# Setup folded into the first units, half groups shifted by one unit, and one PSUM ring of four, in a four-layer graph network on one core

## The reference, cut to what matters

```
x = _layernorm(x + L0(x, adj, W, a_src, a_dst))           # attention, 4 heads: softmax(mask(leaky_relu(si + sj))) @ (xW), elu
x = _layernorm(x + L1(x, adj, weight, w_ih, w_hh, b...))  # 3 rounds: m = h @ weight[i]; aggr = A^T m; h = gru_cell(aggr, h)
x = _layernorm(x + L2(x, adj, weight, bias))              # for r in 1..4: (adj == r) @ x @ weight[r], summed, + bias
x = _layernorm(x + L3(x, adj, W, a))                      # attention, 1 head, elu
```

## Time and profile before

| what | value |
|---|---|
| median of 3 runs | 2815.49 us (2813.47 to 2816.87) |
| the profiled execution, its own time | 2813.75 us |
| its span in the trace | 2811.9 us |
| TensorE: busy, share, matmuls | 2686.6 us, 96%, 15577 |
| VectorE / ScalarE / GpSimd busy | 76% / 59% / 45% |
| mean granted TensorE clock | 0.975 |

### The profile page before, as it was taken

The page is one execution under the profiler, slowest core; times in us unless marked ns, Lnnn a source line. Parts: engine busy times, 40 slices in busy tenths (PEclk is TensorE's granted clock), DMA queues, the critical chain, the costliest instruction groups (busy, mean ns, idle before and its releaser), DMA issues.

```text
span 2811.9 us, 48614 instructions
## 1 busy us (share of the span) xinstructions
PE 2686.6 (96%) x15577; PEld 2315.8 (82%) x15577; DVE 2126.9 (76%) x5138; ACT 1663.4 (59%) x4164; POOL 1257.9 (45%) x1351
## 2 busy tenths in 40 slices
PE   3799999999999999999999999999999999999984
PEld 2678888888888888888888888888888888888873
DVE  6466787777788777878778777877777788777754
ACT  0455666666566666666566666656666666666542
POOL 0134544454445445444544544444444444444442
PEclk8699999999999999999999999999999999999995
DMA  7000000000000000000000000000000000000000
GB/s 202 19 20 18 18 24 22 27 24 26 22 21 24 22 28 24 26 22 18 27 22 27 24 26 18 22 24 26 27 24 24 20 22 22 28 28 18 13 10 16
DMA packets 97276, 75.29 MB, mean 27 GB/s; under 512 B 6624, under 2 KB 92768, under 8 KB 96992
## 3 DMA queue, kind: packets, MB, share of 16 engines
q1 hardware_dynamic: 77296, 54.28, 6.7%
q10 hardware_dynamic: 19696, 17.44, 1.9%
...
## 4 chain that ended last, share of the span: by engine, by line
PE 75%; DVE 11%; issue 4%; ACT 2%; POOL 2%; POOLq 0%; DVEq 0%; ACTq 0%
PE psum L757 45%; PE psum L618 9%; PE psum L674 5%; PE psum L654 3%; PE psum L792 3%; PE psum L745 3%; PE psum L744 2%; PE psum L663 2%; PE psum L633 2%; DVE ht_h L1085 2%; DVE y_t L1031 2%; DVE stats L1008 2%; DVE y_t L1132 1%; ACT x L932 1%; DVE moments L1012 1%
## 5 line engine op out<-in xcount | busy, mean ns | idle before, releaser
L1166 POOL TENSOR_SCALAR rstd<-moments 128x2 f32<-128x2 f32 x256 | 78.8, 308 | 999.5 <-DVE moments L1012 999.1
L757 PE MATMUL psum<-ht_h,whh_h 128*128 128x512 f32 x1152 | 481.3, 418 | 0.0
L757 PE MATMUL psum<-ag_h,wc_h 128*128 128x512 f32 x1152 | 478.2, 415 | 0.0
L757 PE MATMUL psum<-ht_h,whh_l 128*128 128x512 f32 x1152 | 456.0, 396 | 0.0
L757 PE MATMUL psum<-ag_l,wc_h 128*128 128x512 f32 x1152 | 455.6, 395 | 0.0
L757 PE MATMUL psum<-ht_l,whh_h 128*128 128x512 f32 x1152 | 455.5, 395 | 0.0
L757 PE MATMUL psum<-ag_h,wc_l 128*128 128x512 f32 x1152 | 454.1, 394 | 0.0
L1221 POOL TENSOR_TENSOR ht<-ht,g_n 128x512 f32<-128x512 f32 x192 | 265.2, 1381 | 151.2 <-ACT g_n L920 148.7
L757 PEld LDWEIGHTS psum<-ht_h,whh_l 128*128 128x128 f32 x1152 | 216.6, 188 | 52.8
L757 PEld LDWEIGHTS psum<-ag_h,wc_l 128*128 128x128 f32 x1152 | 216.3, 188 | 53.0
L757 PEld LDWEIGHTS psum<-ht_l,whh_h 128*128 128x128 f32 x1152 | 217.7, 189 | 38.6
...
## 6 DMA issues: line engine op xcount, KB each, us to landing
adj_i<-in_adj_dram SPq DMA_DIRECT2D x128, 128.0 KB, 2.1
...
```

The source lines that it names most:

```text
L757: last = mm(dst, s, m, start=(first and k == 0), stop=(last_part and k == len(flat) - 1))
```

## The change

- **Setup.** The separate block is gone. Its loads, transposes, products and splits are steps (`prep_*`, `load_*`, `scan`, `flag`, `learn`) of the same list as everything else. They use banks 4 to 7 before the GRU does (ring `prep`). The products are cut into pieces of one bank. `adj` is scanned in 32 pieces instead of 8, with a ring of 3 buffers; 7 of the pieces stand ahead of the first GRU step, 25 behind it. The flag is worked out and read just ahead of the first `rel_rest`.
- **Halves.** Half k holds units 2k-1 and 2k instead of 2k and 2k+1. There are 33 halves; the first and the last hold one unit (two graphs), and all their GRU steps work on 256 columns instead of 512.
- **Orders.** `HALF` is a new order of the same steps, and `FIRST` and `LAST` list the steps of the two ends by hand.
- **PSUM.** `light` and `misc` become one ring `light` of four banks, taken in the order of the list.

```diff
-SLOTS = {"light": 2, "misc": 2, "adj": 2, "x": 2, "xt": 1, "wh": 2,
+SLOTS = {"light": 4, "adj": 2, "x": 2, "xt": 1, "wh": 2,
-         "adjg": 1, "nodes": 1, "agg": 1, "adjf": 1, ... "x1": 3}
+         "adjg": 1, "nodes": 1, "agg": 1, "prep": 4, "scan": 3, "adjf": 1, ... "x1": 3}
-    "gru_load": ("adjg",), "gru_nodes0": ("nodes",), "gru_turn0": ("misc",),
-    "gru_agg": ("misc",), "gru_turn": ("misc",), "gru_fin": ("misc", "yf"),
+    "gru_load": ("adjg",), "gru_nodes0": ("nodes",), "gru_turn0": ("light",),
+    "gru_agg": ("light",), "gru_turn": ("light",), "gru_fin": ("light", "yf"),
+    "prep_hh": ("prep",), "prep_ih": ("prep",), "prep_wl": ("prep",), "prep_w3": ("prep",), "prep_mul": ("prep",),
+    "scan": ("scan",), "flag": ("light",),
...
+FIRST = """
+prep_first()  load_first()  pre_load(0)  load_ih()  att_xt(pre,0)  pre_load(1)  att_wh(pre,0,0)  att_wh(pre,0,1)
...
+gru_agg(0,0,0)
+gru_agg(0,0,1)  att_wh(pre,2,0)  att_wh(pre,2,1)  att_scores(pre,2,0)
...
+LAST = """
...
+gru_in(-1,2,1)  rel_y1(-2)  gru_new(-1,2,1)  rel_rest(-2)  att_prob(post,-3)  att_store(post,-4)  gru_fin(-1,0)  rel_norm(-2)
...
-    return [(name,) + kind + (2 * k + a[1],) + a[2:]]
+    u = 2 * k - 1 + a[1]
+    return [(name,) + kind + (u,) + a[2:]] if 0 <= u < 2 * halves - 2 else []
...
-    HALVES = B // 4
+    HALVES, UNITS = B // 4 + 1, B // 2
...
-        LIGHT, MISC = psum[:, 0:2, :], psum[:, 2:4, :]
+        LIGHT, PREP = psum[:, 0:4, :], psum[:, 4:8, :]
...
+        def units(k):
+            return [u for u in (2 * k - 1, 2 * k) if 0 <= u < UNITS]
...
+            def prep_mul(l, j):
+                i = take(pe, "prep", "prep_mul", l, j)
+                prepped(pe, "prep_wl", l)
+                prepped(pe, "prep_ih", j)
+                for n, c in enumerate((j,) if j < C else range(C)):
+                    cols = slice(0, 2 * D) if j < C else slice(2 * D, G3)
+                    dst = PREP[:, i, :] if j < C else PREP[:, i, n * D:(n + 1) * D]
+                    for e in range(C):
+                        last = mm(dst, wlT[:, l, e, c * P:(c + 1) * P], ihT[:, e, cols], start=(e == 0), stop=(e == C - 1))
+                last.then_inc(s_prep_ps, 1)
...
             def gru_hn(k, l, c):
 
                 if l == 0:
-                    pe.wait_ge(s_ht0_l, 2 * k + 2)
+                    if k == 0:
+                        pe.wait_ge(s_prep_lo, len(PIECES))
+                    pe.wait_ge(s_ht0_l, 2 * k + 2)
...
-                accumulate(HN_PS, gate_terms(rows_of(2, c), whh_h, whh_l, ht_h[k % 2], ht_l[k % 2]), True, True).then_inc(s_ph, 1)
+                accumulate(HN_PS[:, nodes_of(k)], gate_terms(rows_of(2, c), whh_h, whh_l, ht_h[k % 2], ht_l[k % 2], nodes_of(k)), True, True).then_inc(s_ph, 1)
```

More of the change, by code:

```diff
@@ L73 @@
 HALF = """
[L74 to L77 removed]
+rel_h1(-2,0)
+gru_z(-1,1,1)
+gru_in(-1,1,1)  rel_split(-2,1)  rel_adjt(-2,1)  rel_y1(-2,0)  rel_rest(-2,0)
+gru_agg(0,0,0)
+gru_agg(0,0,1)  att_scores(pre,1,0,0)  att_scores(pre,1,0,1)  att_store(post,-3,0)
+gru_hn(0,0,0)  rel_norm(-2,0)  gru_new(-1,1,0)  rel_mask(-2,1)
@@ new lines @@
+gru_agg(0,1,0)
+gru_agg(0,1,1)
+gru_hn(0,1,0)  scan(14)  scan(15)
+gru_rzh(0,1,0)  att_norm(pre,2)
+gru_r(0,1,0)
+gru_z(0,1,0)  scan(16)  scan(17)  gru_nodes0(1)  gru_turn0(1,0)
+gru_in(0,1,0)  gru_turn0(1,1)
+gru_hn(0,1,1)  att_scores(pre,3,0)
+gru_rzh(0,1,1)  gru_n(0,1,0)  gru_new(0,1,0)
+gru_r(0,1,1)
+gru_z(0,1,1)  att_scores(pre,3,1)
+gru_in(0,1,1)
+gru_agg(1,0,0)
+gru_agg(1,0,1)
+gru_hn(1,0,0)  scan(18)  scan(19)  scan(20)  gru_n(0,1,1)  gru_new(0,1,1)  gru_split(0,1)  att_prob(pre,3)
+gru_rzh(1,0,0)  pre_load(4)
@@ new lines @@
+gru_in(1,1,0)
+gru_hn(1,1,1)
+gru_rzh(1,1,1)  gru_nodes0(2)  gru_turn0(2,0)  scan(30)  gru_turn0(2,1)  gru_n(1,1,0)
+gru_r(1,1,1)  att_scores(pre,5,0)  scan(31)
+gru_z(1,1,1)
+gru_in(1,1,1)
+gru_agg(2,0,0)
+gru_agg(2,0,1)  att_scores(pre,5,1)  rel_split(0)  rel_adjt(0)
+"""
+LAST = """
+rel_mask(-4)  gru_new(-2,1,0)
+gru_hn(-1,0,0)
+gru_rzh(-1,0,0)
+gru_r(-1,0,0)  gru_n(-2,1,1)  gru_new(-2,1,1)
+gru_z(-1,0,0)
+gru_in(-1,0,0)
+gru_hn(-1,0,1)
+gru_rzh(-1,0,1)  rel_norm(-5)  att_xt(post,-5)  gru_split(-2,1)  rel_h1(-4)
@@ L132, in placed, with from_end @@
     k = t + a[0]
-    if not 0 <= k < halves:
-        return []
     if name.startswith("gru"):
-        return [(name, k) + a[1:]]
-    return [(name,) + kind + (2 * k + a[1],) + a[2:]]
+        gone = name in ("gru_turn", "gru_fin", "gru_norm") and (k, a[-1]) in ((0, 0), (halves - 1, 1))
+        return [] if gone or not 0 <= k < halves else [(name, k) + a[1:]]
+    u = 2 * k - 1 + a[1]
+    return [(name,) + kind + (u,) + a[2:]] if 0 <= u < 2 * halves - 2 else []
 def program_order(halves):
-    return [s for t in range(-2, halves + 3) for step in half_steps(HALF) for s in placed(step, t, halves)]
+    def from_end(step):
+        name, a = step[0], step[1:]
+        at = 1 if name.startswith("att") else 0
+        return (name,) + a[:at] + (a[at] + (halves if name.startswith("gru") else 2 * halves - 2),) + a[at + 1:]
+    first, last = steps_of(FIRST), [from_end(s) for s in steps_of(LAST)]
+    apart = set(first) | set(last)
+    middle = [s for t in range(-2, halves + 3) for step in steps_of(HALF) for s in placed(step, t, halves)]
+    scans = [("scan", i) for i in range(SCANS) if ("scan", i) not in apart]
+    out = []
+    for s in middle:
+        if s == ("rel_rest", 0) and ("flag",) not in apart:
+            out += [("flag",), ("learn",)]
+        if s not in apart:
+            out.append(s)
+            if s[0] in ("gru_hn", "gru_rzh", "gru_r", "gru_z") and scans:
+                out.append(scans.pop(0))
+    assert not scans
+    return first + out + last
 def bass_gnn_stack(nc, x, adj, L0_gnn_W, L0_gnn_a_src, L0_gnn_a_dst, L1_gnn_weight, L1_gnn_w_ih,
@@ L727, in gru_turn0 @@
             def gru_turn0(k, c):
-                i = take(pe, "misc", "gru_turn0", k, c)
-                pe.wait_ge(s_x1, 2 * k + 2)
-                for q in range(4):
-                    last = turn(MISC[:, i, q * P:(q + 1) * P], x1[k % 3][:, q, c * P:(c + 1) * P], ident[:])
+                i = take(pe, "light", "gru_turn0", k, c)
+                pe.wait_ge(s_x1, units(k)[-1] + 1)
+                for q in each(k):
+                    last = turn(LIGHT[:, i, q * P:(q + 1) * P], x1[k % 3][:, q, c * P:(c + 1) * P], ident[:])
                 last.then_inc(s_turn_ps, 1)
             def gru_agg(k, l, c):
-                i = take(pe, "misc", "gru_agg", k, l, c)
+                i = take(pe, "light", "gru_agg", k, l, c)
                 if l == 0:
```

742 lines of the change are left out of this document (444 added, 298 removed).

## The result

The changed kernel takes 2707.7 us (median of 4 runs, 2705.6 to 2710.0) where the kernel before takes 2814.9: ratio 0.9619, 95% interval 0.9602 to 0.9635. The forecast was 2727 with a range of 2698 to 2768: the sign and the range hold, and the forecast is 19 us too high. The result lies just outside the band of 2708 to 2748 that had a chance of 0.57, on the side of rival F (about 2697). All three parts erred the same way.

What follows compares the result with a forecast made beforehand. TensorE was taken as the bound, 96% busy, with idle time mostly before and behind the GRU. Head 54 + 2622 between the points + tail 49 = 2725, plus 1.85 outside: 2727 us, range 2698 to 2768.

Steps and rivals of the forecast that it cites:

- rival F: Whole kernel, better than forecast: head 46, ramp 4, nothing lost in the middle, tail 44, about 2697 us; chance 0.12.
- The head: Start to the GRU's first matmul: 54 us instead of 115.4, by PE's bound of 6.5 + 48, mostly at low clock.
- Between the points: From the GRU's first matmul to its last: added work, ramp, middle waits and closing part give 2622 us, 2628 before.
- hidden stall: Middle: part of a stall hides in overlapping busy spans; 4 us taken off over 31 periods, 0 to 8.
- late bank: Middle: a bank of the ring of four comes late; 2.5 us of waits left of 9.7, ends 0 and 12.
- ramp and closing part: PE idle at both ends of the GRU stretch: ramp 11 us instead of 6.4, closing 6 instead of 8.2.
- Rival C: Half-wide matmuls at the price of their weight load: 2756 us; chance 0.03.
- Grouping: Middle: 18 runs of transposes a period instead of 21, 0.11 us per transpose and no rest, so worth nothing.
- The tail: From the last GRU matmul to the end: 2.7 + 8.2 + 33.8 + 4, 49 us instead of 69.
- B: Middle: ring of four makes a GRU aggregate wait for scores or moments, +31 us, 2763 or less; chance 0.12.
- A: Head won by half: setup delays units 0 and 1, PE at low clock; first point 72, ramp 28, 2762; chance 0.13.
- D: Slower: bank waits at several places of the period, three stalls of 1.25 us, 116 us more, 2843; chance 0.03.

Runs made afterwards that it cites:

- runs 6: The changed kernel with the whole setup, all 32 scan pieces, flag and learn put ahead of unit 0: 2768.6 us, ratio 0.9828 to the kernel before.
- run 7: The changed kernel with the 25 later scan pieces, flag and learn moved to just ahead of the first gru_agg: 2739.2 us, ratio 0.9726 to the kernel before.
- run 3: The kernel before with one rel_h1 moved a gate product earlier, nothing else: 2801.3 us, ratio 0.9946.
- run 1: The changed kernel in its own order, with two rings of two banks instead of one of four: 2711.7 us, ratio 0.963 to the kernel before.
- run 10: The kernel before with one rel_h1 a gate product earlier and the first att_scores moved behind the next gate product: 2831.7 us, ratio 1.0057.
- run 2: The kernel before in its own order, with one ring of four banks instead of two rings of two: 2830.9 us, ratio 1.0054.
- run 8: The changed kernel with post_load(-1), the loads for the last unit's relation, some 15 us earlier: 2707.9 us, ratio 0.9618 to the kernel before.
- run 5: The changed kernel without the closing list (LAST empty), the last half still half as wide: 2721.7 us, ratio 0.9663 to the kernel before.
- run 4: The changed kernel with the old list of the middle, its ring of four, head and tail orders kept: 2753.6 us, ratio 0.9777 to the kernel before.

## Why the prediction was right, and what it had wrong

**The head, 49.1 for 54: the level of the clock was the term that failed.** I took PE's bound: a start at 6.5 and 48 us of work, "mostly at the low level", with no waits. PE started at 8.9, was busy 9.7 + 24.9 = 34.5 us, and waited 5.7 between. So the work was 13.5 us too high and start and waits 8 too low: that 54 came within 5 us of 49.1 is in part luck. The level rises after the first products of unit 0 (PE's timeline of after):

```profile
8.90 1.09 PE L741 MATMUL psum<-ident,x_in 128*128 128x128 f32 x4 [8.90 <-DMA x_in<-in_x_dram]
12.33 0.56 PE L724 MATMUL psum<-w_h,xt_h 128*128 128x264 f32 x1 [2.34 <-DVE xt_l L1213]
12.69 0.42 PE L724 MATMUL psum<-w_l,xt_h 128*128 128x264 f32 x1
12.91 0.42 PE L724 MATMUL psum<-w_h,xt_l 128*128 128x264 f32 x1
...
16.67 0.60 PE L741 MATMUL psum<-ident,x_in 128*128 128x128 f32 x4
17.11 1.47 PE L682 MATMUL psum<-ident,ih_raw 128*128 128x128 f32 x12
```

Matmuls of 264 columns start 0.22 us apart at 13 us, 0.12 in the steady part; four transposes take 1.09 at 8.90 and 0.60 at 16.67; twelve take 1.47 where the earlier trace rows have 2.79. So half speed (1.2 GHz) held for 8 us of a start that waited until 8.90, not for 40. From 24 us on PE is busy 24.86 of 25: by then it was PE's bound, as I chose it, at 2.4 GHz. Before, waits lay between the setup's transposes, and all of them up to 24 us ran at half speed. VectorE was busy 22.7 of those 25 us (91%), also as forecast. Over the whole head neither reached the 75% that I had named: PE was busy 34.5 us of it (70%), VectorE 32.0 (65%). That most of the gain is overlap, runs 6 and 7 show.

**Between the points, 2614.3 for 2622: two terms, errors against each other.** I took 9.7 - 2.5 + 4 = 11.2 us off for the waits of the middle, and it was 25. The step that failed is the 4 us for a hidden stall over 31 periods: shown idle was 0.35 us a period, and the period fell by 0.96. I had written that busy spans overlap the following start, and then left it at a small number. The 2.5 us for a late bank didn't come either. Start to start, the place of the earlier trace rows alone loses about 0.5 us a period, and run 3 got 0.49 back. Of the other 0.47, run 1 gives 0.10 to the ring and 0.37 to the rest of the order. Part of it is a second hidden stall, ahead of the first scores, which run 10 was to price and missed; the trace of run 2 has the answer. The scores take the bank of `rel_y1`, which VectorE's `y_t` empties (the kernel before, then run 2, the same list with four banks):

```profile
1073.90 0.69 DVE L1059 TENSOR_TENSOR y_t<-psum,x 128x512 f32<-128x512 f32 x1 [0.72 <-issue]
...
1074.37 0.28 PE L745 MATMUL psum<-edges,hn_l 128*128 128x128 f32 x1
1074.64 0.65 PE L654 MATMUL psum<-ident,wh 128*128 128x128 f32 x4
```
```profile
1078.69 0.28 PE L745 MATMUL psum<-edges,hn_l 128*128 128x128 f32 x1
1078.81 0.61 PE L654 MATMUL psum<-ident,wh 128*128 128x128 f32 x4
```

The two starts are 0.27 us apart before, 0.29 in the mean of 25 periods; in run 2, in run 1 and in after they are 0.11 apart. So 0.17 us a period was a wait for a bank, and either the ring or the new order ends it. The remaining 0.3 us no run took apart.

On the other side ramp and closing part. I took 11 and 6 us of idle time against 6.4 and 8.2 before, and with 3 us of added work the ends were to cost 5.4 us more; they cost 12.0. The idle time came out near the forecast in sum, with errors against each other: 5.5 us from 49 to 298 for 11, and 10.3 from 2414 to 2663 (9.1 of it from 2600 on) for 6. What I had left as it was is the clock. It is granted 0.90 from 49 to 100, 0.98 from 140 to 217 and 0.86 from 2600 to 2663; the same 63 us before the last gate matmul had 0.95 in the kernel before, and 115 to 160 had 0.84. That makes about 31 us at half speed between the two points against about 20, so up to 5 us more, an estimate from the granted shares. It also differs between executions: run 8, with 0.93 and 1.00 where after has 0.90 and 0.98, is the one that takes 246.7 us for 249.2, with the same idle time. The rest of the 12.0 no run takes apart.

**Half-wide matmuls: right.** Gate matmuls of 256 columns at the end start 2663.15, 2663.27, 2663.39, so 0.12 apart, while the weight load's rows show 188 to 189 ns. Rival C did not happen.

**Grouping worth nothing: nothing found against it.** Eight transposes take 0.88 us (2414.41 to the next step at 2415.29), twice the 0.45 of four. (The trace has 17 runs of transposes in the new period, not 18.)

**The late weights and the scan at no cost, 2 us for the flag: right.** No wait of PE for either of the first two is shown, and the flag costs 0.2 + 1.9 us (run 7 above shows the rows).

**The tail, 44.8 for 49: the mechanism right, three terms oversized by a little.** From the last gate matmul to the last unit's `rel_h1` it takes 13.5 us (2663.39 to 2676.92), where I had 2.7 + 8.2 and the 4 for the company of units 61 and 62, so 14.9. From there it is 31.3 us for 33.8. One unit's chain is left, and PE is busy 19.7 of 46 us. Run 8 shows that a wait of 4 us in PE's row there is not on it. Run 5 gives the own order's part: without it the closing stretch takes 9.6 us more and the tail 2.9. With 47.7 us its tail is still 21.6 shorter than before. What run 5 has there and the kernel before hasn't is the narrow last half, so that is the likely cause; no run took it away alone.

**The rivals.** B needs both the ring of four and the old list: run 2 has it at 16 us, run 4 has it too, and the new list has none. There the two aggregates of that round stand apart, and VectorE reaches the first one's low part as soon as ScalarE has the high part (VectorE and PE in the timeline of after):

```profile
1072.42 0.69 DVE L1343 TENSOR_TENSOR ag_l<-psum,ag_h 128x512 fp32r<-128x512 f32 x1 [0.58 <-ACT ag_h L1066]
...
1074.49 0.60 PE L763 MATMUL psum<-ident,wh 128*128 128x128 f32 x4
```

The bank is free at 1073.11, 1.4 us ahead of the second scores; in run 2 the same `ag_l` ended after PE had begun to wait. I weighed B by PE's distances alone and gave it 0.12; the two lists on VectorE would have told that the new one has no such place. A fell with the clock. D's price of 2.8 us a period was never near: both old stalls together make 1.41. Two of the rivals' sums don't come out. B's 31 us, with the 9 already off in the forecast, give 2758 and not 2763. F's terms (8, 7, 2.5 and 5 us) give 2704.5 and not 2697, so the measured 2707.7 lies nearer to F than F's number says.
